# A two-layer adaLN block on one core: opening of the first layer rebuilt, two ScalarE steps moved, the first layer's experts written out

## The reference, cut to what matters

```python
h = _layernorm(x) * (1 + ca) + sa                 # ca, sa, ga: one row per batch
Q, K, V = proj(Wq, bq), proj(Wk, bk), proj(Wv, bv)   # 16 heads of 8; Q, K scaled to length 1
attn = softmax(Qn @ Kn.T / sqrt(8))
g1 = gelu(h @ Wg1.T + bg1, approximate=False)     # 64 hidden channels
gate_dynamic = sigmoid((g1 @ Wg2.T + bg2).mean(axis=1))   # one number per batch and head
x = x + ga * ((attn @ V * sigmoid(g) * gate_dynamic) @ Wo.T + bo)
h = _layernorm(x) * (1 + cb) + sb
# 4 experts, 128 -> 256 -> 128, weights dense_w per token from a softmax over 1 to 4 kept
x = x + gb * sum_e dense_w[:, e] * (relu(h @ ew1[e] + eb1[e]) @ ew2[e] + eb2[e])
```

## Time and profile before

| | us |
|---|---|
| median of three | 1929.44 (1929.28 to 1932.81) |
| the profiled execution, its own time | 1927.27 |
| its span, first to last instruction | 1925.5 |
| PE busy | 1601.8 (83%) |
| DVE busy | 1276.2 (66%) |
| ACT busy | 1158.1 (60%) |
| POOL busy | 895.3 (46%) |
| one group of the experts, from PE's turn of the weights to the next | 14.54 |
| a piece of x, from issue to landing, median of 8 | 8.9 |
| a transfer that fills the routing table, from issue to landing, median of 8 | 32.9 |

### The profile page before, as it was taken

One profiled execution on the slowest core, in us unless ns is written; L12 is line 12 of the kernel. 1 busy time (PEld: TensorE's weight loads), 2 busy tenths in 40 slices (PEclk: granted clock), 3 DMA queues, 4 the chain that ended last, 5 costly groups with the idle time before them and its releaser, 6 DMA issues.

```text
span 1925.5 us, 39513 instructions
## 1 busy us (share of the span) xinstructions
PE 1601.8 (83%) x12775; PEld 816.7 (42%) x12775; DVE 1276.2 (66%) x3330; ACT 1158.1 (60%) x1846; POOL 895.3 (46%) x1715
## 2 busy tenths in 40 slices
PE   1979989999987699895999999999999822999970
PEld 1843333333333233332444444444444421676750
DVE  6545666666664777774676667766676662777757
ACT  1446677777765678882556556565565451887750
POOL 2333444454441133332444343865737653666664
PEclk9999999999998899996999899999998955999995
DMA  6012112112110892002222122322312132222228
GB/s 192 1 30 36 37 34 34 42 37 34 34 34 12 321 386 101 0 1 71 48 40 48 34 46 39 69 61 47 67 39 58 42 122 92 88 89 85 90 68 261
DMA packets 234360, 142.85 MB, mean 74 GB/s; under 512 B 183938, under 2 KB 201346, under 8 KB 233156
## 3 DMA queue, kind: packets, MB, share of 16 engines
q1 hardware_dynamic: 222464, 120.67, 23.9%
q0 software_dynamic: 9088, 18.89, 3.0%
q10 hardware_dynamic: 2628, 1.00, 0.2%
HBM read 38.64 MB, written 59.90 MB: 51 GB/s over the span
## 4 chain that ended last, share of the span: by engine, by line
PE 36%; issue 11%; DVE 10%; POOL 3%; POOLq 3%; ACT 2%; DVEq 1%; DMA 1%; SPq 1%; ACTq 0%
PE OP L2162 7%; PE OP L2336 5%; PE SP L2321 5%; DVE mx L1336 4%; PE M L2125 4%; PE M L2100 2%; PE SP L2142 2%; POOLq L656 2%; PE M L2116 2%; PE M L2121 2%; POOL h_dram L484 2%; PE OP L2174 1%; PE M L2311 1%; DVE sq L1649 1%; POOLq L262 1%
## 5 line engine op out<-in xcount | busy, mean ns | idle before, releaser
L872 ACT ACTIVATE pt<-SP 128x768 f32<-128x768 f32 x256 | 207.4, 810 | 256.2 <-PE SP L2142 255.0
L1336 DVE TENSOR_REDUCE mx<-M 128x2 f32<-128x512 f32 (+1 forms) x384 | 257.7, 682 | 111.8 <-PE M L2125 108.8
L523 POOL TENSOR_SCALAR_AFFINE_SELECT pt<-pt 128x256 f32<-128x256 f32 x512 | 199.1, 413 | 271.8 <-ACT pt L872 269.9
L764 ACT ACTIVATE pt<-SP 128x1024 f32<-128x1024 f32 x256 | 258.0, 1021 | 35.5 <-PE SP L1905 32.9
L554 POOL DMA_INDIRECT y_dram<-hT,dest x156 | 150.3, 963 | 113.3 <-DVE hT L1629 76.8
L1924 PE MATMUL OP<-pt,vs 128*32 128x256 f32 x1408 | 185.4, 385 | 0.0
L970 ACT ACTIVATE pt<-SP,b 128x512 f16<-128x512 f32 x156 | 107.3, 688 | 87.7 <-PE SP L2321 61.6
L484 POOL DMA_INDIRECT h_dram<-hT,slot x128 | 130.1, 1016 | 57.9 <-issue 31.7
L2162 PE MATMUL OP<-pt,vs 128*32 128x128 f32 (+1 forms) x1408 | 152.3, 338 | 5.1 <-POOL pt L523 5.1
L1623 DVE TENSOR_TENSOR pt<-vs,pt 128x512 f16<-128x512 f32 x156 | 107.8, 691 | 56.5 <-ACT vs L971 56.5
L653 POOL TENSOR_TENSOR st<-st,ksT 128x512 f32<-128x512 f32 x48 | 71.4, 1487 | 152.9 <-DVE ksT L1754 152.8
(11 more groups left out here) (325 smaller groups left out, 3388.6 us busy)
## 6 DMA issues: line engine op xcount, KB each, us to landing
h_dram<-shared SPq DMA_DIRECT2D x8, 4488.0 KB, 32.9
hT<-h_dram SPq DMA_DIRECT2D x39, 264.0 KB
rows<-g_dram SPq DMA_DIRECT2D x4, 2048.0 KB, 7.1
pt<-y_dram SPq DMA_DIRECT2D x32, 256.0 KB, 3.5
x_sb<-in_x SPq DMA_DIRECT2D x8, 512.0 KB, 8.9
pt<-in_w SPq DMA_DIRECT2D x4, 1024.0 KB, 5.3
out<-x_sb SPq DMA_DIRECT2D x16, 256.0 KB, 3.0
y_dram<-hT,dest POOLq DMA_INDIRECT x156
```

The lines of the kernel that those rows point to most:

```text
L523: last = pool.affine_select(out=diag, in_=diag, compare_op=ALU.is_ge, fill=0.0, base=0, pattern=[[0, 2], [1, P]], channel_multiplier=-1)
L764: act.activation(pt[:, u % 4], SP[u % 2][:], ACT.Exp, scale=SCALE).then_inc(s["exp"], 1)
L872: act.activation(pt[:, u % 4, :, 0:384], SP[u % 2][:, :, 0:384], ACT.Exp, scale=SCALE).then_inc(s["exp"], 1)
L1336: dve.tensor_reduce(to, M[:, k % 2, :].rearrange("p (j k) -> p j k", j=4 if k < 4 else 2), AX.X, ALU.max).then_inc(s["mred"], 1)
```

## The change

Opening:
- The gate's first layer is computed with its 64 channels in partitions: one matmul of `wx[0]` (64 columns) against the 256 tokens of `hT`. The bias is then one number per partition, and Gelu adds it and sums over the tokens into `gsum` (`accum_out`). The bias addition on DVE, the sum on PE and its copy go; ACT writes `hT` itself, and POOL's `keep` goes.
- The loop is written out. Statistics are made for 16 tiles first, then batches 0 to 7 run (`HEAD`), then the statistics of the other 48 tiles, then batches 8 to 31. Between these the chains of batches 0 to 2 (`project`, `take`, `square`, `lengths`, `unit`, `high`, `low`) are set.
- ACT's splitting of the expert weights moves behind the last Gelu, ahead of the sigmoid; POOL's part moves into the first four batches of the dense loop. DVE's tables and bias rows move behind the last normalisation. PE no longer waits for the gains before the loop, but PE's first score now waits for `gl_in` (the gate's logits), as its first projection did before. On SP the transposes of batch 0 stand, as before, behind the transfers of the gate.

```diff
@@ weights' staging
+        HEAD = 8
             if l == 0:
-                at = (0, 512, 1024, 4096)[c]
-                return shared[:, at:at + COLS[0] // 2]
+                at = (1536, 7424, 0, 512)[c]
+                return (shared[:] if c < 2 else ksT[:].rearrange("p a j t -> p (a j t)").bitcast(F32))[:, at:at + COLS[0] // 2]
@@ gpsimd
-            weight_low(0)
...
-                def one(b, par):
-                    pool.wait_ge(s["h"], b + 1)
-                    pool.tensor_tensor(hT[:, bass.ts(b, T)], hcur[:, par, :], one_s[:, 0:T],
-                                       ALU.mult).then_inc(s["hT"], 1)
...
+                    if b < CHUNKS:
+                        weight_low(b)
...
-                    pool.tensor_copy(ccur[l][:, par],
-                                     comb3[l][:, bass.ts(g, GT)].rearrange("p t r e -> p t (r e)")).then_inc(s["c"], 1)
...
-                with pool.Fori(1, NG // 2 - 1) as i:
-                    for par in range(2):
-                        one(2 * i + par, par)
+                for g in range(NG):
+                    one(g, g % 2)
@@ scalar
+            def norm(b):
+                act.wait_ge(s["zT"], b + 1)
+                act.activation(hT[:, b * T:(b + 1) * T], bank[b % 2][:, 0:T], ACT.Identity,
+                               bias=modT[0][:, SA, b:b + 1], scale=modT[0][:, CA, b:b + 1]).then_inc(s["h"], 1)
+            def gate(b):
+                act.wait_ge(s["x"], b + 1)
+                act.activation(gact[:, b % 2], bank[2 + b % 2][0:HID, 0:T], ACT.Gelu, bias=bx[0][:, 0:1],
+                               accum_out=gsum[:, b:b + 1]).then_inc(s["gelu"], 1)
+            def gates(n):
+                if n:
+                    gate(n - 1)
+                if n < B:
+                    norm(n)
...
+                steps = [(square, 0), (square, 1), (high, 0), (square, 2), (high, 1)]
+                for n in range(HEAD, B + 1):
+                    gates(n)
+                    k = n - HEAD
+                    if k % 4 == 1 and k // 4 < 5:
+                        step, b = steps[k // 4]
+                        step(b)
+                for c in range(CHUNKS):
+                    weight_high(0, c)
+                sigmoid()
                 for b in range(B):
                     exp(b, 0)
                     exp(b, 1)
+                    exp(b, 2)
                     if b + 2 < B:
                         high(b + 2)
-                    exp(b, 2)
                     exp(b, 3)
+                    exp(b, 4)
                     if b + 3 < B:
                         square(b + 3)
-                    exp(b, 4)
@@ vector
+            conditions()
+            first_stats(range(2))
             dve.drain()
+            statistics(slice(0, 16))
+            modulations()
+            for b in range(HEAD):
+                ln(b)
+            first_stats(range(2, 8))
             dve.drain()
+            statistics(slice(16, NT))
...
+                steps = {1: [(take, 0)], 3: [(lengths, 0)], 5: [(take, 1)], 7: [(lengths, 1)], 8: [(unit, 0)], 10: [(low, 0)],
+                         12: [(take, 2)], 14: [(lengths, 2)], 16: [(unit, 1)], 18: [(low, 1)]}
+                for n in range(HEAD, B):
+                    ln(n)
+                    for step, b in steps.get(n - HEAD, []):
...
+                    if n - HEAD == 6:
+                        gains()
+                dve.drain()
+                bias_rows()
+                blanks()
+                static_gate()
@@ tensor
+            def norm(b):
+                pe.wait_ge(s["z"], b + 1)
+                if b >= 2:
+                    pe.wait_ge(s["h"], b - 1)
...
+            def gate(b):
+                pe.wait_ge(s["h"], b + 1)
+                if b >= 2:
+                    pe.wait_ge(s["gelu"], b - 1)
+                pe.matmul(bank[2 + b % 2][0:HID, 0:T], wx[0][:], hT[:, b * T:(b + 1) * T],
+                          start=True, stop=True).then_inc(s["x"], 1)
+            def gates(n):
+                if n < B:
+                    norm(n)
+                if n:
+                    gate(n - 1)
...
+                for n in range(HEAD, B + 1):
+                    gates(n)
+                    k = n - HEAD
+                    if k in (0, 4, 11):
+                        for t in range(TT):
+                            project((0, 4, 11).index(k), t)
+                pe.wait_ge(norm_s[0]["gelu"], B)
+                pe.wait_ge(g_fin, 1)
+                pe.matmul(bank[4][0:B, 0:H], gsum[:], wg2[:], start=True, stop=True).then_inc(gl_mm, 1)
+                pe.wait_ge(gl_in, 1)
...
-                    pe.wait_ge(s["c"], g + 1)
...
-                                            ccur[l][:, par, t, :], identb[:])
+                                            comb3[l][:, GT * g + t].rearrange("p r e -> p (r e)"), identb[:])
```

321 lines of the change are left out of this document (102 added, 219 removed).

## The result

The changed kernel takes 1876.38 us (median of 4 runs, 1872.27 to 1881.24) beside 1929.36 us (1925.83 to 1932.81, 4 runs) for the kernel before. The ratio is 0.9733, with a 95% interval of 0.9703 to 0.9764. The forecast was 1870, with a range of 1853 to 1886.

The account below looks back on a forecast made before the run. PE, busy 83% of the span, was taken to bound the kernel, waiting for exp in the dense loop and POOL's copy in the experts. Gains of 35.5 + 20.8 + 2.7 = 59.0 us gave 1870.4 us, range 1853 to 1886.

Parts of the forecast that it names:

- Term 1: Dense loop: moving exp 2 ahead of `high` removes PE's waits for exp; gain 35.5 us, between 22 and 40.
- It waits about 0.15 us with the semaphore, for 29 batches 4.4 us: Dense loop: PE's remaining wait at the turn behind ACT's `normal`, taken off the 37.9 us of exp waits.
- `unit` hangs on a transpose early in the batch that nothing moves: Dense loop: reason given why `high` on ACT still starts at 315.37 after the reorder.
- it doesn't come late: Dense loop: POOL's refinement, 0.72 us ahead of `unit`, was to stay on time because `lengths` moves ahead by 1.2 us.
- the rival of the dense wait that moves on: Dense loop: the turn behind `normal`, or POOL's refinement, takes half of the first gain; 1887 us, chance 0.12.
- Term 2: Experts: without POOL's copy PE goes on 1.56 us earlier in a group; gain 20.8 us, between 12 and 21.5.
- Nothing was late next: Experts: claim that ACT, DVE and POOL keep up with 13.0 us for a group instead of 14.54.
- Term 3: Opening: first score at 130.7 instead of 133.44 us; gain 2.7 us, between -5 and 15.
- The round trip: Opening: gate matmul on PE, Gelu and norm on ACT bound each batch at 2.4 us, against 1.85 before.
- The low clock of the opening: Opening: PE was priced at the low level, 1.2 GHz, throughout.
- The rival of the high clock: Opening at 2.4 GHz: gate about 0.6 us less per batch, 14.4 us over 24 batches; 1858 us, chance 0.14.
- The sum: Whole kernel: the three gains, 35.5 + 20.8 + 2.7 = 59.0 us, giving 1870.4 us.

Follow-up runs that it names:

- e1: Kernel before with only two ACT steps of the dense loop moved (`high` behind exp 2, the square behind exp 4); median 1946.5 us against 1968.9, ratio 0.9846.
- after: The changed kernel with all three parts, against the kernel before; median 1876.38 us, ratio 0.9733.
- e12: Changed kernel with opening reordered, its chain shortened, statistics spread, `normal` ahead of `square`, DVE's `unit` and lower halves earlier; median 1822.2 us, ratio to before 0.949.
- e4: Changed kernel with POOL's copy of the routing weights kept, all expert loops written out; profiled span 1892.6 us, experts 248.9 us.
- e5: Changed kernel with the experts' hardware loops and POOL's copy kept, the copy one addition earlier and two groups ahead; profiled span 1865.5 us, experts 228.4 us.
- e3: Kernel before with only the opening rebuilt; ratio to before 1.0029 (0.9984 to 1.0073), first score at 128.4 us.
- e7: Changed kernel with ACT's two opening steps swapped, norm(n) ahead of gate(n-1); profiled span 1855.5 us, first score at 111.4 us.
- e9: The changed kernel run again unaltered; median 1873.2 us, ratio to before 0.9723.

## Why the prediction was right, point by point

- **Term 1, the dense loop: direction and mechanism right, 6 us too much.** Forecast 35.5 us, measured 31.0 alone (e1) and 29.1 in the full change, inside its range of 22 to 40. The waits for exp went as told (37.9 to 0.9 in e1, 1.8 in after), and the clock gave 4.6 (10 us less at the low clock in e1, at 0.46) where I took 2. The size that was wrong is in "It waits about 0.15 us with the semaphore, for 29 batches 4.4 us": it is 10.4 us in e1, in 18 of the batches, up to 1.9 each. I took one batch and let `high` start at 315.37 because "`unit` hangs on a transpose early in the batch that nothing moves". That batch is real: in nine of batches 3 to 29 of the changed kernel (4, 8 and odd ones) `unit` starts on time, PE does not wait at the turn, and the batch takes 13.68 us. In nine of the others POOL's refinement ends less than 0.3 us ahead of `unit`, which then starts up to 0.3 us late and runs 0.2 to 0.4 us longer; e12 shows that the refinement is late because DVE's guess stands behind the wait for the output projection. So "it doesn't come late" was the wrong sentence; the rival of the dense wait that moves on named this refinement, at its right place and with a third of its price.
- **Term 2, the experts: right.** Forecast 20.8 with 0.4 of it ahead of the first group; measured 21.7 and 1.2. A group 12.92 against 13.0. Nothing was late next. That writing out costs and gives nothing, and that the copy's place was the cost, is shown by e4 and e5.
- **Term 3, the opening: mechanism right, 3 us too little.** Forecast 2.7, measured 5.7. The round trip was 2.22 us instead of 2.4: from the gate matmul to Gelu 90.03 - 88.87 = 1.16 us (forecast 1.23), from Gelu with its accumulator to the norm 90.49 - 90.03 = 0.46 (forecast 0.46 to 0.71), from the norm to the next gate matmul 0.60 (forecast 0.56). The first score, forecast at 130.7, came at 127.8, and at 125.5 to 128.7 in the other profiles of the same opening (133.4 to 134.6 in the three with the old one). In the total this term was too small to be seen (e3).
- **The low clock of the opening: mostly right.** I forecast the low level throughout. The granted clock is up for 13.7 us in all between 52.9 and 87.0, and of the 32 gate matmuls 24 take 1.11 or 1.12 us and 7 take 0.65. By the rule of the Trainium skill ("TensorE: Matmul & The Clock Gate", What's actually happening) activity releases the throttle; the rises and falls of e7 agree with it, the rows of the opening before, busy and slow from 50 to 122 us, do not. What sets the two apart, no run here shows. The rival of the high clock was priced too high: at 2.22 and 1.75 us for a batch, 24 batches with the clock up would have given 0.47 each, about 11 us (an estimate), not 14.4.
- **The sum.** 59.0 forecast for the four stages, 57.7 measured: the terms' errors were -6.4, +2.1 (with the stretch ahead of the experts) and +3.0. That they cancel to 1.3 is luck; each lies inside the range given for its term or, for the experts, 1.4 above it. The profiled execution then lost 12.2 us in the second layer's attention, which no term held. In the medians the gain is 53.0 us (56.1 in e9), so 1870.4 was 3 to 6 us too low. The forecast had no term for the clock of stages that the change does not touch; two profiles of one program show that it moves the dense loop by 7 us and the attention by 16. Either is more than the 3 to 6 us by which the forecast missed.

## What to carry to other kernels

When a wait on the busiest engine is removed, the next limit is the chain that ended just in time before: follow the one with the least spare back to the engine that starts it, over several batches, and ask what that engine stands waiting for with ready work behind it. Here it was DVE, at a wait whose own lateness cost nothing, and putting ready work ahead of that wait (together with the early `unit`) was worth 9.7 us, some 8 without the clock. A loop over two engines that hand one item back and forth costs the whole round trip; issuing the next item's first step ahead of this item's last one adds no work, and here the first score came 14 to 17 us earlier, with the matrix engine at the higher clock for more of the time.

## What the runs showed of the hardware that was not expected

- TensorE's clock fell from 2.4 to 1.2 GHz in the midst of dense work: PE was busy 14.26 of the 15 us ahead of the fall at 1055 us and had 1.2 GHz for 13.7 us then. In the middle of the second layer's attention it happened not at all in three profiles, once in eight, twice in two and four times in one; two profiles of the same program had four and one. Each us at the low level went with 0.39 us there and 0.46 in the dense loop.
- In the opening of the kernel before, the granted clock reads 1.00 while the matmuls have the lengths of the low level. In the changed kernel, too, it reads 1.00 up to 52.9 us beside gate matmuls of 1.12 us. Up to its first change the lengths are the better witness.
- On one of the chips the last part of the kernel, from the end of the second attention, took 420 to 431 us instead of 380, in three kernels alike, with every other stage unchanged; the excess is in the second layer's expert blocks (284.5 to 294.1 us instead of 245.1).
- A Gelu with a sum over the row takes 0.47 us and 0.19 us for `ACTIVATION_READ_ACCUMULATOR`, and the next activation starts 0.09 us behind the start of the latter.
